# An experts layer moved into the attention of the next image, with diagonal tiles spread and GpSimd's sums on VectorE

## The reference

```python
def _ln_t(v): ...            # (v - mean) / sqrt(var + 1e-5), over the 128 channels of a token

def _L3_attn_ref(x, W1, b1, w2, b2):          # W1 (256, 16), w2 (16, 1)
    f = einsum('bih,ha->bia', x, W1[:128]); g = einsum('bjh,ha->bja', x, W1[128:])
    t = tanh(f[:, :, None, :] + g[:, None, :, :] + b1)
    scores = einsum('bija,a->bij', t, w2[:, 0]) + b2[0]
    e = exp(scores) * tril(ones, -1)          # key j strictly before query i
    w = e / (sum(e, axis=-1, keepdims=True) + 1e-10)
    return einsum('bij,bjh->bih', w, x)

def _L3_ffn_ref(x, router_w, router_b, expert_w, expert_b):   # 8 experts, 2 chosen
    top_p, top_i = top_k(softmax(x @ router_w + router_b), 2)
    top_p = top_p / sum(top_p)
    expert_out = einsum('bnd,edc->bnec', x, expert_w) + expert_b
    return einsum('bnk,bnkc->bnc', top_p, take(expert_out, top_i))

t = t + _L3_attn_ref(_ln_t(t), ...)
t = t + _L3_ffn_ref(_ln_t(t), ...)
x = transpose of t back to (4, 128, 64, 64)
```

## Time and profile before

| | us |
|---|---|
| median of 3 runs | 8764.21 (8760.24 to 8766.25) |
| the profiled execution | 8764.93 |
| its span in the trace | 8763.1 |
| busy PE, DVE, ACT, POOL over the span | 6793.0, 6439.3, 5612.2, 2881.3 |
| attention loop, from the first fill to the last exp | 4314 to 8367 |
| experts of layer 3 | 8379 to 8707 |
| turn back to channels | 8707 to 8763 |

### The profile page before, as it was taken

How to read it: one execution, slowest core, us unless ns; L and a number is a source line. 1 busy time by engine, 2 the same in 40 slices (tenths; PEclk the granted TensorE clock), 3 DMA queues, 4 the chain that set the end, 5 groups by cost and what they waited for, 6 DMA issues and landing times. The chain is left out here.

```text
span 8763.1 us, 103094 instructions
## 1 busy us (share of the span) xinstructions
PE 6793.0 (78%) x37512; PEld 2460.3 (28%) x37512; DVE 6439.3 (73%) x10840; ACT 5612.2 (64%) x4625; POOL 2881.3 (33%) x2218
## 2 busy tenths in 40 slices
PE   8999999987886169948876767777777767767688
PEld 3333333323443123314321213221222212212144
DVE  6777777776754643357888888888888888888766
ACT  3222222214554342234699999999999999999954
POOL 5655566630000300005431223231322223213255
PEclk9999999987887579978989999999999999999998
DMA  1000000001010000000000000000000000000000
GB/s 47 1 1 1 1 1 1 1 4 27 23 26 4 7 0 0 0 0 3 3 1 1 1 1 1 1 1 1 1 1 1 1 1 1 1 1 1 1 3 39
DMA packets 23728, 45.12 MB, mean 5 GB/s; under 512 B 10219, under 2 KB 13421, under 8 KB 22127
## 3 DMA queue, kind: packets, MB, share of 16 engines
q1 hardware_dynamic: 23278, 39.11, 1.5%
HBM read 13.92 MB, written 8.39 MB: 3 GB/s over the span
## 5 line engine op out<-in xcount | busy, mean ns | idle before, releaser
L2350 ACT ACTIVATE aa_tanh<-aa_tanh 128x4096 f32<-128x4096 f32 (+8 forms) x1280 | 3699.3, 2977 | 133.5 <-DVE aa_tanh L2479 133.3
L2479 DVE TENSOR_SCALAR aa_tanh<-aa_f_times,aa_g_bias 128x1024 f32<-128x1024 f32 (+19 forms) x5120 | 3307.6, 718 | 634.2 <-PE aa_scores L2389 633.2
L2389 PE MATMUL aa_scores<-aa_tanh,aa_w_spread 128*32 128x512 f32 (+8 forms) x18432 | 2204.7, 596 | 997.3 <-ACT aa_tanh L2350 996.4
L2318 POOL TENSOR_TENSOR aa_denominators<-aa_denominators,aa_weights 128x1024 f32<-128x1024 f32 (+7 forms) x304 | 771.1, 2536 | 2132.5 <-ACT aa_weights L2341 2122.8
L2389 PEld LDWEIGHTS aa_scores<-aa_tanh,aa_w_spread 128*32 128x32 f32 x18432 | 598.0, 113 | 2454.0 <-ACT aa_tanh L2350 1533.3
L278 POOL TENSOR_TENSOR near_tap_weights<-near_hat_y_mask,near_hat_x 128x1024 f32<-128x1024 f32 x400 | 937.6, 2367 | 473.8 <-PE near_weights_spread L570 465.2
L584 PE MATMUL near_out_sum<-near_weighted,near_w_out 128*128 128x512 f32 x1984 | 997.9, 626 | 24.4 <-DVE near_weighted L357 13.9
L570 PE MATMUL near_weights_spread<-near_tap_weights,near_spread_consts 36*64 36x512 f32 x6272 | 799.3, 609 | 19.3 <-DVE near_weighted L357 12.9
L2403 PE MATMUL aa_out_sum<-aa_weights,aa_normed 128*128 128x512 f32 (+3 forms) x1152 | 598.7, 641 | 148.7 <-POOL aa_weights L2313 148.7
L346 DVE TENSOR_TENSOR near_weighted<-near_weights_spread,near_values 128x1024 f32<-128x1024 f32 x496 | 589.5, 1220 | 147.4 <-PE near_weights_spread L570 147.4
L346 DVE TENSOR_TENSOR near_weights_spread<-near_weights_spread,near_values 128x1024 f32<-128x1024 f32 x288 | 354.0, 1229 | 336.9 <-PE near_weights_spread L570 336.9
(11 more groups left out here) (332 smaller groups left out, 7239.2 us busy)
## 6 DMA issues: line engine op xcount, KB each, us to landing
l_taps<-l_scan_in_out SPq DMA_DIRECT2D x256, 64.0 KB, 2.0
x_rows<-in_x SPq DMA_DIRECT2D x4, 2048.0 KB, 14.3
out_x<-x_rows SPq DMA_DIRECT2D x4, 2048.0 KB, 6.3
qa_x<-in_L_attn_w SPq DMA_DIRECT2D x1, 1024.0 KB, 5.7
L_ffn_expert_w<-in_L_ffn_expert_w SPq DMA_DIRECT2D x2, 512.0 KB
near_spread_consts<-in_deform_consts SPq DMA_DIRECT2D x1, 805.5 KB, 8.2
aa_weights_in<-in_attention SPq DMA_DIRECT2D x1, 577.5 KB
l_weights<-in_mamba SPq DMA_DIRECT2D x1, 557.0 KB
```

The costliest lines, as they stand in the source:

```text
L2318: pool.tensor_tensor(DEN[:, lo:CHUNK], DEN[:, lo:CHUNK], ET[:, n % 2, 0:w], ALU.add).then_inc(den_added, 1)
L2350: a.activation(TH[:, tt, 0:length], TH[:, tt, 0:length], ACT.Tanh).then_inc(th_ready, 1)
L2389: last = t.matmul(sp_[32 * q:32 * q + 32, n % 2, s:e], W2S[:, tt, :], TH[:, tt, o + s:o + e], start=tt == 0, stop=tt == 3, tile_position=( ...
L2479: last = v.tensor_scalar(TH[:, tt, at[q]:at[q] + w - s], FR[:, m % 2, lo + s:CHUNK], GB[:, key:key + 1], None, ALU.add)
```

## The change

1. Layer 3's experts for images 0 to 2 are computed inside the attention block of the next image (`attention_and_experts`). The work of an image is cut into eight groups of four tiles (`G`). Each group has a fixed list of jobs that go through the same two banks: a transpose (`mt`), logits (`ml`), eight expert products of half a tile's experts (`e`: two a tile, four experts each), and a transpose back to channels (`x`). One job stands behind a quarter of a full, non-diagonal tile, a group to every 11 such quarters with two groups under way, from the fifth tile of a chunk to its last five. The 18 gating steps stand at five of these quarters, with 4 tiles (32 columns) at a time; ScalarE's exp for the gates stands at another. VectorE adds all eight experts. The norm's factors are made per image, with a square root on ScalarE at the second chunk of images 1, 2 and 3. SyncE sends an image out when its last group is turned.
2. `moe_layer` and `to_channels` at the end handle the last image alone (32 tiles, 4 passes).
3. The order of key tiles changes (`key_order`): the diagonal ones stand between the others, every c+1-th tile, and in the first chunk wide and narrow ones alternate. Where a tile is narrower than 512 columns, the exp of the tile before comes behind its fourth tanh.
4. Masks and sums of the denominators (`add_denominators`) go from GpSimd to VectorE, two tiles behind the fills. Jobs are emptied by VectorE one tile behind TensorE's.
5. Three more transfers load the experts' weights and biases at the start of the attention.

The diff, cut to its core:

```diff
-def moe_layer(nc, d, T, C, N, tag, last_norm):
+def moe_layer(nc, d, T, C, N, tag, last_norm, first=0):
...
-        NCK, NGRP = TT // CK, TT // 4
+        NTL = TT - first
+        NCK = NTL // CK
...
+GE = 4 * EX
+STEPS, PERIOD = 18, 11
+NGI = NT // 4
...
-        tiles = [(m, j) for m in range(NM) for j in range((m % NCH + 1) * CT_)]
+        def key_order(c):
+            if c == 0:
+                return [0, 7, 1, 6, 2, 5, 3, 4]
+            order = list(range(c * CT_))
+            for k in range(CT_ - 1, -1, -1):
+                order.insert(min(c * k + 1, 7 * c), c * CT_ + k)
+            return order
+
+        tiles = [(m, j) for m in range(NM) for j in key_order(m % NCH)]
...
+        def own_job(n, tt):
+            m = tiles[n][0]
+            i, s = n - first_of[m], (m % NCH + 1) * CT_ - 5
+            name, at = None, m - 1
+            if m:
+                name = {(1, 1): "den", (2, 0): "out0", (2, 2): "out1"}.get((i, tt))
+            if m + 1 < NM and name is None:
+                name, at = {(s, 0): "turn0", (s, 2): "turn1", (s + 1, 0): "f0", (s + 1, 2): "f1", (s + 2, 0): "g"}.get((i, tt)), m + 1
...
+        behind, choose, raise_gates = {}, {}, {}
+        for b in range(NB - 1):
+            at = [(n, tt) for n, (m, j) in enumerate(tiles) for tt in range(4)
+                  if m // NCH == b + 1 and j < m % NCH * CT_ and 4 <= n - first_of[m] < (m % NCH + 1) * CT_ - 5]
+            for g in range(NGI):
+                G, p = b * NGI + g, PERIOD * g
+                behind[at[p]], behind[at[p + 3]] = ("mt", G), ("ml", G)
+                for k, o in enumerate((1, 2, 4, 5, 7, 8, 9, 10)):
+                    behind[at[p + PERIOD + o]] = ("e", 8 * G + k)
+                behind[at[p + 2 * PERIOD + 6]] = ("x", G)
+                for o, steps in ((4, range(0, 4)), (5, range(4, 8)), (6, range(8, 12)), (9, range(12, 15)), (10, range(15, STEPS))):
+                    choose[at[p + o]] = (G, steps)
+                raise_gates[at[p + 8]] = G
...
         @block.gpsimd
...
-            def add_denominators(n):
...
             for n in range(len(tiles)):
-                add_denominators(n)
...
+                for tt in range(4):
+                    name, G = behind.get((n, tt), (None, 0))
+                    if name == "mt" and G % NGI < NGI - 1:
+                        normalize_group(G + 1)
...
         @block.scalar
...
-                    if n and tt == 2:
+                    if n and tt == (2 if w >= BANK else 3):
                         exponents(n - 1)
+                    if (n, tt) in raise_gates:
+                        a.wait_ge(diff_ready, 1 + raise_gates[n, tt] + 1)
+                        a.activation(M1[:, :], M2[:, :], ACT.Exp).then_inc(raised, 1)
+                    if m > NCH and m % NCH == 1 and j == 0 and tt == 1:
+                        N.scalar(a, vv, ss, m // NCH, (m // NCH - 1) * NT, m // NCH * NT)
...
         @block.tensor
...
+            def experts(E):
+                G, k, h = E // 8, E % 8 // 2, E % 2
+                t.wait_ge(*bank_before("e", E))
+                t.matmul(bank("e", E), MT[:, G % 2, k * P:(k + 1) * P], EWC[:, 4 * h:4 * h + 4, :].rearrange("p e c -> p (e c)"), start=True, stop=True).then_inc(full("e", E)[0], 1)
...
         @block.vector
...
+            def add_denominators(n):
+                m, j, diagonal, lo, w = shape(n)
+                v.wait_ge(e_ready, 1 + n + 1)
+                if diagonal:
+                    v.tensor_tensor(ET[:, n % 2, 0:P], ET[:, n % 2, 0:P], C["strict"], ALU.mult).then_inc(masked, 1)
+                    v.wait_ge(masked, 1 + diagonals[n])
+                if n:
+                    v.wait_ge(den_added, 1 + n)
+                if j:
+                    v.tensor_tensor(DEN[:, lo:CHUNK], DEN[:, lo:CHUNK], ET[:, n % 2, 0:w], ALU.add).then_inc(den_added, 1)
...
+            def add_experts(E):
+                G, k, h = E // 8, E % 8 // 2, E % 2
+                x = T[:, (4 * G + k) * P:(4 * G + k + 1) * P]
+                v.wait_ge(*full("e", E))
+                if h:
+                    v.wait_ge(*free("e", E - 1))
+                for e in range(4):
+                    c = k * EX + 4 * h + e
+                    ins = v.scalar_tensor_tensor(x, bank("e", E)[:, e * P:(e + 1) * P], GT_[:, G % 2, c:c + 1], x, ALU.mult, ALU.add)
+                    if e < 3:
+                        sum_ch(ins)
+                    else:
+                        ins.then_inc(free("e", E)[0], 1)
...
                 for tt in range(4):
                     fill(n, tt)
+                    if n >= 2 and tt == 2:
+                        add_denominators(n - 2)
+                    if m and (i, tt) == (2, 0):
+                        keep_out(m - 1)
...
+                    name, at = behind.get((n - 1, tt), (None, 0))
...
+                    elif name == "e":
+                        add_experts(at)
...
+                    G, steps = choose.get((n - 1, tt), (0, ()))
+                    for step in steps:
+                        gating(G, step)
...
-        additive_attention_layer(nc, d, X, C, N)
-        moe_layer(nc, d, X, C, N, "L3_ffn_", False)
-        to_channels(nc, X, C, out)
+        attention_and_experts(nc, d, X, C, N, out)
+        moe_layer(nc, d, X, C, N, "L3_ffn_", False, TT - NT)
+        to_channels(nc, X, C, out, NB - 1)
```

More of the change, by code:

```diff
@@ L1998, in _ @@
                 normalize(g)
-            for t in range(TT):
+            for t in range(NTL):
                 c, k = slot(t)
@@ L2402, in add_tile @@
                     if s0 < (h + 1) * BANK:
-                        last = t.matmul(op[:, s0:(h + 1) * BANK], UN[:, j * P:(j + 1) * P], ET[:, n % 2, s0 - lo:(h + 1) * BANK - lo], start=j == 0, stop=diagonal and lo == (h + 1) * BANK - P)
+                        last = t.matmul(op[:, s0:(h + 1) * BANK], UN[:, j * P:(j + 1) * P], ET[:, n % 2, s0 - lo:(h + 1) * BANK - lo], start=j == 0, stop=n == closes(m, h))
                 last.then_inc(o_done, 1)
@@ L2537, in _ @@
+            add_denominators(len(tiles) - 2)
+            add_denominators(len(tiles) - 1)
             keep_out(NM - 1)
@@ L2541, in _, with to_channels @@
             v.wait_ge(st_ready, 1 + 2 * NM)
-            N.vector(v, Chain(v, c2), vv, ss)
-def to_channels(nc, T, C, out):
+            N.moments(v, norm_ch, vv, (NB - 1) * NT, TT)
+            N.factors(v, norm_ch, ss, NB, (NB - 1) * NT, TT)
+def to_channels(nc, T, C, out, image):
     with stage_semaphores(nc, "out_") as sem, ExitStack() as ctx:
```

302 lines of the change are left out of this document (225 added, 77 removed).

## The result

| | before | after |
|---|---|---|
| median of 6 runs, us | 8764.1 (8760.2 to 8768.6) | 8724.1 (8718.4 to 8728.8) |
| ratio, 95% interval | | 0.9954 (0.9942 to 0.9966) |
| the profiled execution, its span | 8764.9, 8763.1 | 8722.6, 8720.8 |
| experts of layer 3 at the end: to the first expert sum, from there | 31 + 297 | 32 + 69 |
| turn back to channels | 54 | 19 |

The account below looks back on a forecast made before the run. ScalarE was taken to bound the attention before, VectorE the stretches with expert jobs after. Terms: -223 - 35 + 135 + 11 + 14 + 4 + 2 + 3 = -89, from 8764.9 to 8676 us; range 8585 to 8770.

Parts of the forecast that it names:

- Experts at the end, -223: Last experts layer: 96 of 128 tiles, at 2.32 us each, leave the end, -223 us.
- Turn back, -35: Turn to channels at the end: 12 of 16 passes of 2.88 us go, -35 us.
- Expert work inside, +135: Attention, images 1 to 3: VectorE is late where jobs are packed into full tiles, about 45 us per image, +135.
- the small terms: ScalarE's small exps and square roots +14, input transfers +4, a full last attention tile +2, GpSimd's normalisations +3 us.
- Masks and sums, 0: Attention: on VectorE they cost 340 us, about even with 280 us freed by faster fills; ScalarE sees neither, 0.
- Diagonals spread, +11: Attention: narrow tiles between full ones lose 134 us in all, where 123 were lost before, +11.
- Where VectorE is late anyway they hide: Narrow tiles' losses vanish in late stretches, leaving 38 us in image 0 and 32 in each of images 1 to 3.
- The price of one narrow tile: Attention: a narrow tile between full ones loses 4.8, 3.2 or 1.7 us, near 10 a chunk together.
- Rival 3: Late stretches: TensorE's jobs wait for banks that VectorE frees late; 264 jobs stall, 8808 at 0.5 us each; chance 0.10.
- Rival 1: Attention: four tanh buffers and diagonals' light moments carry the jobs, ScalarE never starves; 8541 us, half 8608; chance 0.15.
- Rival 2: Attention: 96 normalisations each hold VectorE about 0.44 us, +42, 8718; or jobs cost 30% more, +41; chance 0.22 together.

Follow-up runs that it names:

- e6: e1 with each of the 192 jobs inside the attention adding two of its four experts: 8550.9 us.
- e7: e1 with a group of expert work to every 15 quarters instead of 11: 8597.4 us.
- e12: e7 with the gates' exp later, next chunk's preparing jobs earlier, jobs also beside the two widest diagonal tiles, a group to every 17 quarters: 8558.5 us.
- e4: The kernel before with the new key tile order and masks and sums on VectorE, experts at the end: 8843.7 us.
- e13: e1 with the masks back on GpSimd, sums still on VectorE: 8631.8 us.
- e9: The changed kernel with the masks back on GpSimd, sums still on VectorE: 8674.6 us.
- e8: The changed kernel with the first chunk of each image alone in rising order: 8690.3 us.
- e1: The changed kernel with key tiles in rising order again, the exp always behind the third tanh: 8653.3 us.
- e15: e12 with the next chunk's preparing jobs back where the change has them and masks on GpSimd: 8524.0 us.
- e2: The kernel before with only the new key tile order and exp place, masks and sums on GpSimd, experts at the end: 8920.8 us.

## Why the prediction was right or wrong

- **Experts at the end, -223: right.** From the first expert sum (8631.3) to the last addition (8699.8) 68.5 us are left of 297: -228. **Turn back, -35: right.** It went from 53.8 us to 19.3.
- **Expert work inside, +135, and the small terms: right when taken together.** The moved experts bring 120 us in both rows of the table; with the 228 + 35 that left the end, their cost inside is 143, against 135 + 14 + 4 + 3 = 156. That VectorE is the bound there is what e6, e7 and e12 show: take work from it or thin it, and the time follows. The chunks with most of the jobs, the third and fourth of images 1 to 3, were idle 27 to 31 us each, in e4, without the jobs, 9 to 13.
- **Masks and sums, 0: nearly right, but by luck.** Together +8 in rising order. I asked only how much VectorE time they take, and the mask's cost lies in when it comes: 22 us in rising order, 50 in the changed kernel (e13, e9; of the 50 some 8 are VectorE's own time, 0.29 for each of 9 masks in the late stretches of three images). The prediction names the chain ("a diagonal's tile sum waits for the third fill of the following tile") but as half of a rival, not in the sum.
- **Diagonals spread, +11: the step that failed.** It measured +71 (+70 without experts). The forecast took 9.7 us for each of the sixteen chunks, 155 in all, let 21 of them hide behind VectorE's lateness, and set the 134 that were left against 123. It failed in two places. First chunks: they were costed like any other, and in e4 they lose 13 to 21 us each, 71 in place of 39. There narrow and wide tiles alternate with no full tile between, and the late mask holds TensorE: 27 us of idle go with rising order there (e8), 32 with the masks on GpSimd (e9). "Where VectorE is late anyway they hide": in sum nothing hid, since the experts cost the same 120 us in either order. It was true of the third chunks alone (30.1 and 29.7 against 36.3 in e1); the fourth ones of images 1 and 2 are 5 us worse (27.3 against 22.3), the last chunk 15 (31.3 against 16.4). The other twelve chunks of e4 lose 125 us, near the 116 that the forecast gave them.
- **The sum with what was measured:** -228 - 35 + 143 + 8 + 71 = -41, against the -40 of the result.
- **The price of one narrow tile was right at full clock:** 1.7, 3.2 and 4.8 us were forecast for 384, 256 and 128 columns, and 1.7, 3.05 and 3.9 stand in the third chunk of image 1 in e4. The forecast took TensorE's scores and sum at 1.92 and 1.98 us, what they take in a full loop; at a lower granted clock they took up to 2.76 and 3.78, and the 256 wide tile cost up to 4.7.
- **Rival 3** had the mask in it, which was real, but put the wait at the banks. In the whole attention TensorE's matmuls waited under 40 us for banks and 220 for masks (its weight loads under 70 and 291). Such a total is not a price: in e1 the matmuls waited 176 us for masks, and taking the masks away gained 22 (e13).
- **Rival 1** (the lead absorbs all) is out for this kernel, as idle rose by 194 us. e15, with rising order, masks on GpSimd and thinner jobs together, has the idle time that it forecast.
- **Rival 2** (port) is out: queued full fills beside a normalisation of either kind start 0.69 us apart (101 of them), others 0.66 (2510), so the normalisations cost VectorE about 3 us, not 42. That the result, 8724, lies near this rival's 8718 is chance. GpSimd pays, 836 ns each where one alone takes 440:

```profile
L2402 POOL TENSOR_SCALAR aa_group_normed<-x_rows,norm_scale,aa_shift_plus 128x128 f32<-128x128 f32 x96 | 79.0, 836 | 2488.2 <-PE aa_turned L2528 1767.9
```

The Trainium skill, SBUF — State Buffer, section Who interferes with whom, has it that where the two want the shared ports, whichever comes second is fully blocked; beside normalisations these rows show that on GpSimd's side alone. Beside GpSimd's two-operand sums the trace comes nearer to it: three fills beside one took twice as long in e2 (4.18 us).

- **Range and chances.** 8585 to 8770 held the time, but by luck: its upper end came from rivals 2 and 3, not from a dearer spread, and the forecast's own band, 8630 to 8705 with a chance of 0.53, was missed by 19 us. Faster by more than 17.5 us was given 0.84, and it is faster by 40.

Open: what decides whether the clock falls at a narrow tile (it did in some chunks and not in others of the same order) was not tried, so how much of the spread's 70 us is the clock's is known for single tiles only, about 1.5 us each time. The second chunks' 9.7 to 10.1 us in e4 were not looked into.

## What to carry to other kernels

When an engine takes over small work, ask first who waits for it and where in its new queue it stands; the time it takes comes second. Give extra work to the engine that is second busiest only as thin as its slack per loop turn allows, here a group to 17 quarters instead of 11, and do not break a run of short iterations up: a short iteration covers little, and here every place where it met a long one was a wait of its own. Measure each part of a bundled change alone and in pairs; here one part cost 70 us and another saved 120, and the sum hid both.
